# One graph-transformer kernel: joining, first norm and expert gate as one pipeline over groups of 500 nodes

## The chip, the cores and the metric

The kernel runs on one core of a Trainium2 chip. Time is the device time of one execution in microseconds, the median of several runs. The core's engines run side by side, each through its own list of instructions in order, and meet through semaphores: PE (TensorE, matrix products), DVE (VectorE), ACT (ScalarE), POOL (GpSimd; here it issues indirect DMAs) and SP (SyncE; it issues the plain DMAs).

## What is computed

3125 nodes of 256 features, 50,000 edges, two layers. Each layer adds a graph part, a mixer and a feed-forward part:

```python
xn = _layernorm(x)
x = x + _L0_gnn_ref(xn, src, dst, ...) + _L0_mix_ref(xn[None], ...)[0]   # segment_max over edges; attention and MLP
x = x + _L0_ffn_ref(_layernorm(x)[None], Wr, br, W1, ..., bo)[0]         # 8 experts, softmax gate
xn = _layernorm(x)
x = x + _L1_gnn_ref(xn, edge_index, ...) + _L1_mix_ref(xn[None], ...)[0] # 3 SAGE layers; linear attention
x = x + _L1_ffn_ref(_layernorm(x)[None], ...)[0]
```

The expert part is `w = softmax(feat @ Wr + br)`, three matrices W1, W2, Wo for each expert with relu between, and a sum over the experts weighted by w. The change lies between the end of the edge maxima and the experts.

## The kernel before

It is written in stages. Each stage is a `Scope` with a `Block`, in which every engine has its list; at its end all engines meet (L82 clears semaphores and is a barrier). Activations lie transposed, features on partitions: `c.xT`, `c.yn`, `c.a` are 128 x 2 x 3136 floats. `c.a` holds a term of the graph part and is free after the join; its two halves are then used as `c.yh` and `c.yl`, the high and low float16 part of the normalised rows in `c.yn`. A product in three float16 passes (`product3`, L814) reads these halves; `product` (L854) is a plain float32 product.

`join_max` (L713) gathers, for 25 blocks of 125 nodes, the running maxima at each node's last edge from DRAM: 25 indirect DMAs of POOL into 25 slots of `m` (L747). PE spreads carried maxima by a one-hot matrix (L795, two PSUM banks in turn), DVE takes the maximum (L773), PE transposes (L810), DVE adds `c.a`, clips and adds into `c.xT` (L785, L787), in groups of 4 blocks (500 nodes, the seventh has one block). The one-hot is made by DVE (L757) from the carry rows (L732, first in SP's queue). SP then loads the gate's and experts' small tensors and W1, W2 as floats (L734, 16 loads of 256 KB). ACT scales W1 to its high half in four pieces (L829), DVE makes the low half (L837).

`norm` (L861), called for n = 1, normalises all of `c.xT` into `c.yn`, with a software pipeline over the seven groups: mean by PE, centring (L937), square (L917), variance by PE, root (L923), reciprocal (L944), spreading by PE (L907), scaling (L949), high half (L926), low half (L954). It loads Wo. `gate` (L957) computes the logits with Wr as the stationary side, adds `br` (L994), turns them to nodes on partitions (L979), takes the softmax, turns back (L985), stores `dram.gate` (L1021) and splits W2 and Wo.

`experts` (L1025) runs 7 tiles of 448 nodes times 8 experts. `norm` 2, `split2`, `mix1` and three `sage` follow.

Beside all of it POOL writes the adjacency matrix of the later SAGE layers: 400 indirect DMAs, one for a column of cells (`place_cells`, L697, instruction L706). The calls hand fixed ranges to the stages: 0 to 8 in the join, 8 to 40 in norm 1, 40 to 64 in the gate, 64 to 330 in the experts, 330 to 350 in norm 2, 350 to 400 in mix1. A stage ends when its range is issued; the first `sage` needs all 400. DVE counts equal cells for this (L681), in the edge stage and in the experts.

## Time and profile before

| | |
|---|---|
| median of 3 runs | 2274.82 us (2274.58 to 2283.3) |
| profiled execution | 2287.81 us, span 2286.0 us |
| mean granted TensorE clock in it | 0.849 |
| busy share of the span: PE, DVE, ACT, POOL | 76%, 57%, 26%, 51% |
| DMA, mean rate over the span | 100 GB/s |

The profile is one execution recorded by the hardware. Times in it count from the span's start. A row of the order of time gives an instruction's start, its duration, the engine, the line, output and inputs, and in brackets how long the engine had stood and what released it. Edges and first mixer take the first 706 us, the part between them and the experts about 160, the experts about 450, norm 2 to mix1 about 145, the SAGE layers and the last feed-forward part the rest.

### The profile page before, as it was taken

What the parts mean: (1) busy time and instruction counts of PE and PEld (TensorE: products, weight loads), DVE (VectorE), ACT (ScalarE), POOL (GpSimd) and SP (SyncE); (2) the same over time, 40 slices, a digit from 0 to 9 for tenths busy, and PEclk for the clock granted to TensorE, in tenths of its full rate; (3) what the DMA queues carried; (4) which work ended last, traced back from release to release, by engine and by line L of the source; (5) the groups of instructions that cost most, each with busy time, mean ns of one, the idle gap of its engine ahead of it and who ended that gap; (6) DMA issues with size and microseconds to landing.
All of it is one profiled execution on the core that took longest, in us unless ns stands there. A gap on an engine that the chain in (4) does not pass through costs nothing. (4 is left out here: it accounts for less than half of the span.)

```text
span 2286.0 us, 25612 instructions
## 1 busy us (share of the span) xinstructions
PE 1742.0 (76%) x8399; PEld 1010.7 (44%) x8399; DVE 1300.6 (57%) x2567; ACT 594.1 (26%) x937; POOL 1173.6 (51%) x888
## 2 busy tenths in 40 slices
PE   7985454635552746999999259699989999997996
PEld 6862122212221513555555138655565556544543
DVE  6878666766775644777777244545541221115995
ACT  4001001100111124666666131321120010003453
POOL 0888888878886777888888857300000000000343
PEclk9557777777785868999999667899999999997998
DMA  6257688887868202111110020154424443531002
GB/s 171 62 141 196 184 222 216 216 228 211 227 191 206 60 2 51 36 34 33 33 33 13 1 66 2 19 124 108 108 50 119 126 96 92 127 79 38 1 7 78
DMA packets 193170, 229.06 MB, mean 100 GB/s; under 512 B 66574, under 2 KB 174178, under 8 KB 187697
## 3 DMA queue, kind: packets, MB, share of 16 engines
q1 hardware_dynamic: 125887, 172.58, 28.2%
q0 software_dynamic: 67200, 55.46, 11.0%
q8 instruction: 42, 0.69, 0.1%
q14 instruction: 41, 0.34, 0.0%
HBM read 148.81 MB, written 78.24 MB: 99 GB/s over the span
## 5 line engine op out<-in xcount | busy, mean ns | idle before, releaser
L706 POOL DMA_INDIRECT adjacency<-all_cell_val,all_cell_idx x400 | 546.3, 1366 | 151.2 <-issue 120.4
L273 POOL DMA_INDIRECT edge_ring<-b_rows,all_src_idx x400 | 523.9, 1310 | 174.3 <-issue 172.5
L1659 POOL TENSOR_TENSOR ffn_hl<-ffn_hid,ffn_hh 128x448 f16<-128x448 f32 x56 | 70.0, 1252 | 737.9 <-ACT ffn_hid L1676 737.9
L1472 PE MATMUL bank<-sage_adj,sage_zh 125*128 125x448 f16 x1050 | 370.1, 352 | 3.4 <-DVE sage_zl L1526 3.4
L1472 PE MATMUL bank<-sage_adj,sage_zl 125*128 125x448 f16 x1050 | 370.0, 352 | 0.0
L526 DVE SCALAR_TENSOR_TENSOR edge_ring<-edge_ring,w_keep 125x256 f32<-125x256 f32 x399 | 192.9, 484 | 142.6 <-DMA edge_ring<-b_rows,all_src_idx 122.3
L1549 DVE TENSOR_TENSOR sage_u<-bank,w_rd 128x448 f32<-128x448 f32 x42 | 26.2, 624 | 236.2 <-PE bank L1477 233.4
L1472 PEld LDWEIGHTS bank<-sage_adj,sage_zh 125*128 125x128 f16 x1050 | 102.6, 98 | 101.8 <-issue 8.0
L1472 PEld LDWEIGHTS bank<-sage_adj,sage_zl 125*128 125x128 f16 x1050 | 102.7, 98 | 99.6 <-issue 5.8
L681 DVE SCALAR_TENSOR_TENSOR edge_junk<-bank,all_key_c,all_later 125x400 f16<-125x400 f32 x232 | 145.6, 627 | 0.0
L820 PE MATMUL bank<-all_a,w_W1h 128*128 (+1 forms) x448 | 122.5, 355 | 25.0 <-ACTq L1115 25.0
L857 PE MATMUL bank<-mix_hn,w_fc 128*128 128x448 f32 x168 | 82.4, 658 | 59.4 <-DVE mix_hn L642 59.4
L857 PE MATMUL bank<-all_yn,w_qkv 128*128 128x448 f32 x56 | 39.1, 872 | 115.2 <-DVE all_xT L648 89.6
L1179 DVE TENSOR_TENSOR experts_h<-experts_h,experts_gb 128x896 f32<-128x896 f32 x56 | 61.2, 1093 | 67.7 <-ACT experts_h L1119 49.0
L917 ACT ACTIVATE norm_sq<-all_yn 128x1000 f32<-128x1000 f32 (+1 forms) x21 | 19.9, 948 | 304.1 <-DVE all_yn L937 298.5
L681 DVE SCALAR_TENSOR_TENSOR experts_junk<-all_key_c,all_later 125x400 f16<-125x400 f32 x168 | 97.5, 630 | 0.0
L1165 DVE TENSOR_TENSOR experts_h1l<-experts_hf,experts_h1h 128x896 f16<-128x896 f32 x56 | 61.2, 1092 | 63.9 <-ACT experts_hf L1119 60.4
L1119 ACT ACTIVATE experts_h1h<-bank,w_shift,w_scale 128x448 f16<-128x448 f32 x112 | 75.0, 720 | 84.9 <-PE bank L820 84.9
L1119 ACT ACTIVATE experts_h<-bank,w_shift,w_scale 128x448 f32<-128x448 f32 x112 | 75.0, 720 | 75.9 <-PE bank L820 64.1
L857 PE MATMUL bank<-all_xT,all_mean_w 128*128 128x500 f32 (+1 forms) x84 | 42.6, 644 | 62.4 <-PEq L82 62.4
L857 PEld LDWEIGHTS bank<-mix_hn,w_fc 128*128 128x128 f32 x168 | 38.7, 235 | 107.0 <-DVE mix_hn L642 68.2
L820 PE MATMUL bank<-experts_hwh,w_Woh 128*128 128x448 f16 x224 | 79.7, 356 | 2.8 <-DVE experts_hwl L1169 2.8
(423 smaller groups left out, 3598.8 us busy)
## 6 DMA issues: line engine op xcount, KB each, us to landing
sage_adj<-adjacency SPq DMA_DIRECT2D x105, 490.0 KB
run_max<-edge_ring SPq DMA_DIRECT2D x40, 1120.0 KB
adjacency<-edge_zero SPq DMA_DIRECT2D x25, 714.0 KB
experts_gb<-gate_rows SPq DMA_DIRECT2D x56, 224.0 KB
edge_ring<-b_rows,all_src_idx POOLq DMA_INDIRECT x400
adjacency<-all_cell_val,all_cell_idx POOLq DMA_INDIRECT x400
sage_adj<-adjacency SPq DMA_DIRECT2D x105, 56.9 KB
run_max<-edge_ring SPq DMA_DIRECT2D x40, 130.0 KB
```

The lines of the kernel that those rows point to most:

```text
L273: nc.gpsimd.indirect_dma_start(ring[:, k % RING, :], None, dram.rows[:, :], bass.IndirectOffsetOnAxis(ap=c.src_idx[:, k:k + 1], axis=0)).t ...
L526: v.scalar_tensor_tensor(ring[:, k % RING, :], last, w.keep[:, k:k + 1], ring[:, k % RING, :], ALU.min, ALU.max).then_inc(scanned, 1)
L681: v.scalar_tensor_tensor(junk, keys, c.key_c[:, at], c.later[:, bass.ds(L - 1 - k, L)], ALU.is_equal, ALU.mult, accum_out=c.cnt[:, at]).th ...
L706: nc.gpsimd.indirect_dma_start(dram.adj_flat, bass.IndirectOffsetOnAxis(ap=c.cell_idx[:, k:k + 1], axis=0), c.cell_val[:, k:k + 1], None). ...
L820: ins = nc.tensor.matmul(out, a, b, start=(start and i == 0), stop=(stop and i == n - 1))
L857: ins = nc.tensor.matmul(out, a, b, start=(k == 0), stop=(k == len(lhs) - 1))
L1119: return a(out, ps[bank][:, 0:T], ACT.Relu, bias=w.shift[:, i, h, e:e + 1], scale=w.scale[:, i, h, e:e + 1])
L1165: v.tensor_tensor(h1l[:, e % 2], hf[:], h1h[:, e % 2], ALU.subtract).then_inc(low1, 1)
L1179: v.tensor_tensor(h2[:, f % 2], h2[:, f % 2], gb[f][:].unsqueeze(1).to_broadcast([P, KH, T]), ALU.mult).then_inc(dm, 1)
L1472: ins = mm(ps[4 * b + h][:, 0:T], z[:, g * JG + j, half(h)], adj[g][:, j, :], start=(g == 0 and j == 0 and z is zh), stop=False)
L1549: step(v.tensor_tensor(u[:, h, :], ps[4 * b + h][:, 0:T], w.rd[:, at], ALU.mult))
L1659: nc.gpsimd.tensor_tensor(hl[:, m, :], hid[:, m, :], hh[:, m, :], ALU.subtract).then_inc(low, 1)
```

## The change

`join_max`, `norm` 1 and `gate` become one stage `join_norm_gate`. It works in turns over the same seven groups of 500 nodes: in turn t, DVE and PE join group t - 1, centre group t - 2 and scale group t - 3. The gathers go into 8 slots, and from gather 8 on POOL waits until the slot's group is turned; two columns of `place_cells` follow each such gather. The normalised rows are kept as halves only, `c.eh` and `c.el`, which lie in `c.yn`'s space; a float32 copy `y` exists for two groups. The logits are computed block by block with the rows as the stationary side, straight onto node partitions, and `br` is added there from a broadcast row. All of W1, W2 and Wo are split in this stage. The ranges of `place_cells` become 0 to 46 (`JOINED`) in this stage, 46 to 290 in the experts, 290 to 320 in norm 2, 320 to 400 in mix1. `norm` also clears the tail of its output.

The new function (semaphores, some tiles and the batch-norm and softmax arithmetic, which are as before, are cut), then the calls:

```diff
+def join_norm_gate(nc, c, dram, w, loads, plan):
+    w.total = 16 * sum(sem is w.loaded for _, _, sem in plan)
+    G4 = -(-NB // 4)
+    size = lambda g: min(4, NB - 4 * g)
+    at = lambda g: slice(4 * B * g, 4 * B * g + size(g) * B)
+    wide = lambda g: size(g) * B
+    MR = 8
+    mats, first, second = loads
+    with Scope(nc, "join") as s:
+        m = s.sb("m", [B, MR, D])
+        hot = s.sb("hot", [NONE + 1, NP])
+        t1 = s.sb("t1", [P, 4 * B])
+        y = s.sb("y", [P, 2, KH, 4 * B])
...
+        parts = first + second
...
+            def _(sp):
...
+                    sp.dma_start(hot[:, 0:N], dram.carry.partition_broadcast(NONE + 1)).then_inc(rows_in, 16)
+                    for to, from_, sem in plan:
+                        sp.dma_start(to, from_).then_inc(sem, 16)
+                    sp.dma_start(br[:], w.br_row.partition_broadcast(B)).then_inc(rows_in, 16)
+                    for n, (to, from_, sem) in enumerate(mats):
+                        if n % 2 == 0:
+                            sp.wait_ge(split_low, n // 2 + 1)
+                        sp.dma_start(to, from_).then_inc(sem, 16)
+                for k in range(2):
+                    sp.wait_ge(w_copied[k], (G4 + 1 - k) // 2)
...
+            def _(pool):
                 for j in range(NB):
+                    if j >= MR:
+                        pool.wait_ge(turned, 2 * ((j - MR) // 4) + 2)
+                    nc.gpsimd.indirect_dma_start(m[:, j % MR, :], None, dram.runs[:, :],
+                                                 bass.IndirectOffsetOnAxis(ap=c.last_idx[:, j:j + 1], axis=0)).then_inc(got[j % MR], 16)
+                    if j >= MR:
+                        place_cells(nc, c, dram, pool, 2 * (j - MR), 2 * (j - MR) + 2)
+                place_cells(nc, c, dram, pool, 2 * (NB - MR), JOINED)
...
+            def _(act):
+                act.wait_ge(w.loaded, w.total)
+                act.wait_ge(eps_ready, 1)
+                for i in range(2):
+                    nc.scalar.activation(w.bn[:, i, 4], w.bn[:, i, 4], ACT.Sqrt, bias=c.eps3[:, 0:1]).then_inc(bn_sd, 1)
+                def highs(n):
+                    src, hi, _, loaded, total = parts[n]
+                    act.wait_ge(loaded, total)
+                    nc.scalar.activation(hi, src, ACT.Copy, scale=WS).then_inc(split_high, 1)
+                for t in range(2, G4 + 3):
+                    g = t - 3
+                    if g >= 0:
+                        act.wait_ge(var_done, g + 1)
+                        if g >= 2:
+                            act.wait_ge(rs_ready, g - 1)
+                        nc.scalar.activation(sd[:, g % 2, 0:size(g)], ps[3][0:B, 0:size(g)], ACT.Sqrt, bias=c.eps5[0:B, 0:1]).then_inc(sd_ready, 1)
+                    highs(t - 2)
+                    if g >= 0:
+                        act.wait_ge(scaled, g + 1)
+                        nc.scalar.copy(c.eh[:, :, at(g)], y[:, g % 2, :, 0:wide(g)]).then_inc(high, 1)
+                    g = t - 2
+                    if g < G4:
+                        act.wait_ge(centred, g + 1)
+                        if g >= 1:
+                            act.wait_ge(var_done, g)
+                        nc.scalar.activation(sq[:, :, 0:wide(g)], y[:, g % 2, :, 0:wide(g)], ACT.Square).then_inc(sq_ready, 1)
+                for n in range(G4 + 1, len(parts)):
+                    highs(n)
+                act.wait_ge(ready, 1)
+                nc.scalar.activation(lg[:], lg[:], ACT.Exp).then_inc(ex, 1)
+                for g in range(1, G4, 2):
+                    act.wait_ge(w_turned, g + 1)
+                    nc.scalar.copy(hot[0:NEXP, at(g)], ps[g][0:NEXP, 0:wide(g)]).then_inc(w_copied[1], 1)
...
             def _(dve):
...
+                v.memset(c.eps3[:], 1e-3).then_inc(eps_ready, 1)
+                v.memset(c.eh[:, :, N:NP], 0.0)
+                v.memset(c.el[:, :, N:NP], 0.0)
+                dve.wait_ge(rows_in, 32)
+                v.memset(hot[:, N:NP], 0.0)
+                v.tensor_scalar(hot[:, 0:N], hot[:, 0:N], c.col[0:NONE + 1, 0:1], None, ALU.is_equal).then_inc(hot_ready, 1)
+                def fold_bn():
+                    dve.wait_ge(bn_sd, 2)
+                    for i in range(2):
...
+                    v.tensor_scalar(w.bo[:], w.bo[:], WS, None, ALU.mult)
+                def lows(n):
+                    src, hi, lo, _, _ = parts[n]
+                    dve.wait_ge(split_high, n + 1)
+                    v.scalar_tensor_tensor(lo, src, WS, hi, ALU.mult, ALU.subtract).then_inc(split_low, 1)
+                for t in range(G4 + 3):
+                    if t < G4:
+                        for j in range(4 * t, 4 * t + size(t)):
+                            dve.wait_ge(got[j % MR], 16 * (j // MR + 1))
+                            dve.wait_ge(spread, j + 1)
+                            v.tensor_tensor(m[:, j % MR, :], m[:, j % MR, :], ps[6 + j % 2][0:B, 0:D], ALU.max).then_inc(masked, 1)
+                    if t >= 3:
+                        g = t - 3
+                        dve.wait_ge(sd_ready, g + 1)
+                        if g >= 2:
+                            dve.wait_ge(rs_spread, g - 1)
+                        v.reciprocal(rs[:, g % 2, 0:size(g)], sd[:, g % 2, 0:size(g)]).then_inc(rs_ready, 1)
+                    if 1 <= t <= G4:
+                        g = t - 1
+                        for h in range(KH):
+                            dve.wait_ge(turned, 2 * g + h + 1)
+                            step(v.tensor_tensor(t1[:, 0:wide(g)], ps[h][:, 0:wide(g)], c.a[:, h, at(g)], ALU.add))
+                            ins = v.scalar_tensor_tensor(c.xT[:, h, at(g)], t1[:, 0:wide(g)], 0.0, c.xT[:, h, at(g)], ALU.max, ALU.add)
+                            if h == 0:
+                                step(ins)
+                        ins.then_inc(joined, 1)
+                    if t == 1:
+                        fold_bn()
+                    if t >= 3:
+                        g = t - 3
+                        dve.wait_ge(rs_spread, g + 1)
+                        for h in range(KH):
+                            ins = v.tensor_tensor(y[:, g % 2, h, 0:wide(g)], y[:, g % 2, h, 0:wide(g)], ps[4][:, 0:wide(g)], ALU.mult)
+                        ins.then_inc(scaled, 1)
+                    if 2 <= t <= G4 + 1:
+                        g = t - 2
+                        dve.wait_ge(mean_done, g + 1)
+                        if g >= 2:
+                            dve.wait_ge(logits, g - 1)
+                            dve.wait_ge(lowed, g - 1)
+                        for h in range(KH):
+                            ins = v.tensor_tensor(y[:, g % 2, h, 0:wide(g)], c.xT[:, h, at(g)], ps[2][:, 0:wide(g)], ALU.subtract)
+                        ins.then_inc(centred, 1)
+                    if t >= 3:
+                        g = t - 3
+                        dve.wait_ge(high, g + 1)
+                        dve.wait_ge(scaled, g + 1)
+                        v.tensor_tensor(c.el[:, :, at(g)], y[:, g % 2, :, 0:wide(g)], c.eh[:, :, at(g)], ALU.subtract).then_inc(lowed, 1)
+                    if t >= 3:
+                        lows(t - 3)
+                    if t >= 8:
+                        lows(t - 1)
+                dve.wait_ge(logits, G4)
+                step(v.tensor_tensor(lg[:], ps[5][0:B, 0:NB * NEXP].rearrange("p (j e) -> p j e", e=NEXP),
+                                     br[:].unsqueeze(1).to_broadcast([B, NB, NEXP]), ALU.add))
...
+                v.tensor_tensor(lg[:], lg[:], wide_mx, ALU.subtract).then_inc(ready, 1)
+                for n in range(G4 + 2, len(parts)):
+                    lows(n)
                 dve.wait_ge(ex, 1)
...
+                v.tensor_tensor(lg[:], lg[:], wide_mx, ALU.mult).then_inc(ready, 1)
+                for g in range(0, G4, 2):
+                    dve.wait_ge(w_turned, g + 1)
+                    v.tensor_copy(hot[0:NEXP, at(g)], ps[g][0:NEXP, 0:wide(g)]).then_inc(w_copied[0], 1)
...
+            def _(pe):
+                def spread_carry(j):
+                    if j >= 2:
+                        pe.wait_ge(masked, j - 1)
+                    nc.tensor.matmul(ps[6 + j % 2][0:B, 0:D], hot[:, B * j:B * (j + 1)], c.carry[:], start=True, stop=True).then_inc(spread, 1)
+                pe.wait_ge(hot_ready, 1)
+                for j in range(4):
+                    spread_carry(j)
+                for t in range(G4 + 3):
+                    if t + 1 < G4:
+                        for j in range(4 * t + 4, 4 * t + 4 + min(2, size(t + 1))):
+                            spread_carry(j)
+                    if t >= 3:
+                        g = t - 3
+                        pe.wait_ge(rs_ready, g + 1)
+                        if g >= 1:
+                            pe.wait_ge(scaled, g)
+                        for j in range(size(g)):
+                            ins = nc.tensor.transpose(ps[4][:, B * j:B * (j + 1)], rs[:, g % 2, j:j + 1].to_broadcast([B, P]), c.ident[0:B, 0:B])
+                        ins.then_inc(rs_spread, 1)
+                    if t < G4:
+                        pe.wait_ge(masked, 4 * t + size(t))
+                        if t >= 1:
+                            pe.wait_ge(joined, t)
+                        for h in range(KH):
+                            for i in range(size(t)):
+                                ins = nc.tensor.transpose(ps[h][:, B * i:B * (i + 1)], m[:, (4 * t + i) % MR, half(h)], c.ident[0:B, 0:B])
+                            ins.then_inc(turned, 1)
+                    if t >= 3:
+                        g = t - 3
+                        pe.wait_ge(scaled, g + 1)
+                        for i in range(size(g)):
+                            j = 4 * g + i
+                            ins = product(nc, ps[5][0:B, NEXP * j:NEXP * (j + 1)], [y[:, g % 2, k, B * i:B * (i + 1)] for k in range(KH)],
+                                          [w.Wr[:, k, :] for k in range(KH)])
+                        ins.then_inc(logits, 1)
+                    if 1 <= t <= G4:
+                        g = t - 1
+                        pe.wait_ge(joined, g + 1)
+                        if g >= 1:
+                            pe.wait_ge(centred, g)
+                        product(nc, ps[2][:, 0:wide(g)], [c.mean_w[:]] * KH, [c.xT[:, k, at(g)] for k in range(KH)]).then_inc(mean_done, 1)
+                    if 2 <= t <= G4 + 1:
+                        g = t - 2
+                        pe.wait_ge(sq_ready, g + 1)
+                        if g >= 1:
+                            pe.wait_ge(sd_ready, g)
+                        for j in range(size(g)):
+                            ins = product(nc, ps[3][0:B, j:j + 1], [sq[:, k, B * j:B * (j + 1)] for k in range(KH)], [c.mean_w[:, 0:1]] * KH)
+                        ins.then_inc(var_done, 1)
+                    if t + 1 < G4:
+                        for j in range(4 * t + 6, 4 * t + 4 + size(t + 1)):
+                            spread_carry(j)
+                pe.wait_ge(ready, 2)
                 for g in range(G4):
+                    for i in range(size(g)):
+                        ins = nc.tensor.transpose(ps[g][0:NEXP, B * i:B * (i + 1)], lg[:, 4 * g + i, :], c.ident[0:B, 0:B])
+                    ins.then_inc(w_turned, 1)...
@@ experts
-                                       [(c.yh[:, k, cols(t)], c.yl[:, k, cols(t)]) for k in range(KH)])
+                                       [(c.eh[:, k, cols(t)], c.el[:, k, cols(t)]) for k in range(KH)])
@@ build
-                join_max(nc, c, dram, w, plan, pieces(f[0], w.W1, mats[0]))
-                norm(nc, c, 1, lambda pool: place_cells(nc, c, dram, pool, 8, 40), [(f[0][:, e], blocks(i.Wo)[:, e], mats[2]) for e in each])
-                gate(nc, c, w, dram, pieces(f[1], w.W2, mats[1]) + pieces(f[0], w.Wo, mats[2]), lambda pool: place_cells(nc, c, dram, pool, 40, 64))
+                join_norm_gate(nc, c, dram, w, ([(f[0][:, e], blocks(i.Wo)[:, e], mats[2]) for e in each],
+                                                pieces(f[0], w.W1, mats[0]) + pieces(f[1], w.W2, mats[1]),
+                                                pieces(f[0], w.Wo, mats[2])), plan)
-            experts(nc, c, w, dram, made, lambda pool: place_cells(nc, c, dram, pool, 64, 330, made))
+            experts(nc, c, w, dram, made, lambda pool: place_cells(nc, c, dram, pool, JOINED, 290, made))
-                norm(nc, c, 2, lambda pool: place_cells(nc, c, dram, pool, 330, 350), [
+                norm(nc, c, 2, lambda pool: place_cells(nc, c, dram, pool, 290, 320), [
-            mix1(nc, c, w, qT, ctx, lambda pool: place_cells(nc, c, dram, pool, 350, L))
+            mix1(nc, c, w, qT, ctx, lambda pool: place_cells(nc, c, dram, pool, 320, L))
```

## Rows read from the trace of the kernel before

**Rows 1.** Busy us by engine (instructions), clock, DMA share, GB/s, one stretch

```profile
1280.00:1328.00 48.00, 0.42 (x1) 0.45 (x2) 0.11 (x2) 0.00 (x0) 34.96 (x30) 0.50 0.07 1
```

**Rows 2.** In order of time: the ends and beginnings of stages

```profile
873.31 0.93 PE L820 MATMUL bank<-all_a,w_W1h 128*128 128x448 f16 x2 [24.95 <-ACTq L1115]
...
1322.61 1.19 POOL L706 DMA_INDIRECT adjacency<-all_cell_val,all_cell_idx  x1 [0.30 <-issue]
...
1327.62 0.08 DVE L931 MEMSET all_a<- 128x22 f16 x1 [51.15 <-PEq L82]
...
1358.01 1.19 POOL L706 DMA_INDIRECT adjacency<-all_cell_val,all_cell_idx  x1 [0.30 <-issue]
...
1365.85 1.48 ACT L829 ACTIVATE w_glh<-staged_gl 128x1536 f16<-128x1536 f32 x1 [1.75 <-PEq L82]
...
1445.38 4.35 POOL L706 DMA_INDIRECT adjacency<-all_cell_val,all_cell_idx  x1 [0.31 <-issue]
...
1473.34 0.29 PE L820 MATMUL bank<-w_glh,all_a 128*125 128x256 f16 x1 [2.27 <-PEq L82]
```

**Rows 3.** The join's start in order of time, then its first stretch by engine

```profile
711.66 0.33 SPq L732 DMA_DIRECT2D all_yn<-carry_of  x1
...
713.70 19.36 SPq L734 DMA_DIRECT2D staged_float<-in_W  x16
...
719.99 1.85 DVE L757 TENSOR_SCALAR all_yn<-all_yn,all_col 126x3125 f32<-126x3125 f32 x1 [8.19 <-DMA all_yn<-carry_of]
...
722.98 0.51 ACT L741 ACTIVATE w_bn<-w_bn,all_eps 128x16 f32<-128x16 f32 x2 [9.82 <-DMA w_bn<-in_bn]
...
711.00:740.00 29.00, 12.55 (x44) 8.11 (x44) 13.20 (x33) 5.69 (x7) 22.37 (x18) 0.62 1.01 247
```

**Rows 4.** In order of time: first maximum and first group's transposes

```profile
726.95 0.73 DVE L773 TENSOR_TENSOR join_max_m<-join_max_m,bank 125x256 f32<-125x256 f32 x2
...
732.87 1.04 PE L810 MATMUL bank<-all_ident,join_max_m 125*128 125x125 f32 x8
```

**Rows 5.** POOL: gathers, their landing, columns by stretch, one column in the gate

```profile
L747 POOL DMA_INDIRECT join_max_m<-run_max,all_last_idx x25: 1207/1211/2220, 712.4 to 750.9; - x25
...
DMA to landing us min/median/max: 4.0/4.3/9.1
...
1276.40:1323.80 47.40, 37.95 (x32) 0.53 0.07 1
...
874.00:1276.40 402.40, 331.06 (x235) 0.99 0.16 33
...
828.86 9.61 POOL L706 DMA_INDIRECT adjacency<-all_cell_val,all_cell_idx  x1 [0.30 <-issue]
```

**Rows 6.** DVE by line, join then norm 1: count, busy us, mean ns, idle

```profile
L773 DVE TENSOR_TENSOR join_max_m<-join_max_m,bank 125x256 f32<-125x256 f32 x25 | 10.1, 418 | 9.2 <-PE bank L795 6.5 <-DMA join_max_m<-run_max,all_last_idx 2.5
L787 DVE SCALAR_TENSOR_TENSOR all_xT<-join_max_t,all_xT 128x500 f32<-128x500 f32 (+1 forms) x14 | 8.7, 624 | 0.5
...
L837 DVE SCALAR_TENSOR_TENSOR w_W1l<-staged_float,w_W1h 128x1024 f16<-128x1024 f32 x4 | 4.9, 1218 | 0.0
...
L937 DVE TENSOR_TENSOR all_yn<-all_xT,bank 128x500 f32<-128x500 f32 (+1 forms) x14 | 8.0, 615 | 5.6 <-PE bank L857 5.6
...
L954 DVE TENSOR_TENSOR all_a<-all_yn,all_a 128x1000 f16<-128x1000 f32 (+1 forms) x7 | 7.5, 1082 | 0.0
```

**Rows 7.** PE in norm 1, in order of time: variance, means, variance again

```profile
779.25 1.80 PE L857 MATMUL bank<-all_mean_w,norm_sq 128*125 128x1 f32 x16
...
781.37 1.84 PE L857 MATMUL bank<-all_xT,all_mean_w 128*128 128x500 f32 x4
...
795.36 3.52 PE L857 MATMUL bank<-all_mean_w,norm_sq 128*125 128x1 f32 x16 [1.97 <-ACT norm_sq L917]
```

**Rows 8.** The gate's end: PE's transposes, and SP's wait for the store

```profile
842.99 5.37 PE L985 MATMUL bank<-all_ident,gate_lg 125*8 125x125 f32 x25 [3.93 <-DVE gate_lg L1006]
...
SPq L969 <- DMA gate_rows<-gate_wT: 2.9, 1, 2.9
```

More of the change, by code:

```diff
@@ new lines, in _ @@
+            @block.sync
+            def _(sp):
+                with nc.allow_non_contiguous_dma(reason="weights in blocks of 128 rows"):
+                    sp.dma_start(hot[:, 0:N], dram.carry.partition_broadcast(NONE + 1)).then_inc(rows_in, 16)
[8 more added lines that the diff above has]
+                    sp.wait_ge(w_copied[k], (G4 + 1 - k) // 2)
+                sp.dma_start(dram.gate[:, :], hot[0:NEXP, :]).then_inc(gate_stored, 16)
+                sp.wait_ge(gate_stored, 16)
```

171 lines of the change are left out of this document (32 added, 139 removed).

## The prediction, made before the change was run

> **What bounds the kernel now.** I read the page's time slices first, then the busy time by stretch, then the order of time around each stage's end. The reader should look for the engine that works last in each stage, because every stage ends in a barrier that all engines must reach. From the first join to the first SAGE layer that engine is mostly POOL, which writes the 400 adjacency columns by `place_cells`. After the experts' compute comes a stretch of 48 us in which PE is busy 0.42 us, DVE 0.11 and POOL 34.96 [rows 1]; POOL's last issue there is at 1322.61, and norm 2's first DVE work at 1327.62 [rows 2]. Norm 1 and the gate end on POOL in the same way. From POOL's last end (1322.61 + 1.19) to the next stage's work I count 3.6 us, rounded down from 3.8 for the stages whose engines start sooner. Norm 2 and mix1 end on compute: POOL is through at 1359.2 and 1449.7, the next stages start at 1365.85 and 1473.34 [rows 2]. So POOL has 400 columns to write between 711.7 and 1473.3, and a compute gain in this part counts only where it isn't behind POOL.
>
> The stretches that the change touches, by their starts: join, norm 1 and gate 711.7 to 873.3, 161.6 us; experts 873.3 to 1327.6, 454.3; norm 2 to 1365.9, 38.3; split2 and mix1 to 1473.3, 107.5.
>
> **Columns moved after the experts.** Columns by stage before and after: join to gate 64 and 46, experts 266 and 244, norm 2 20 and 30, mix1 50 and 80. One column costs 1.49 us where nothing disturbs it (47.4 us for 32) and 1.71 us beside the experts (402.4 us for 235) [rows 5].
>
> Experts: 244 columns. 234 of them fit beside the compute as now, 10 follow: the 22 that go were all in the 47.4 us tail, so 22 x 1.49 = 32.8 us less. Ten columns (14.9 us) still stand behind the compute, so the cut is taken in full. Reading `eh`, `el` out of another buffer costs the experts' matmuls nothing: same shapes, same order.
>
> Norm 2: ten more columns put POOL's end at 1359.2 + 14.9 + 0.5 for DVE's interference = 1374.6 on the old time line, the next stage 3.6 later at 1378.2 instead of 1365.9: +12.3. A 22-column memset is nothing.
>
> Mix1: thirty more put POOL's end at 1449.7 + 44.7 = 1494.4. POOL's column at 1445.38 took 4.35 us, 3.2 over its 1.19, beside a whole-tile DVE subtraction (L1299) [rows 2]; the product of the same shape at L1304 now also meets columns. Between 0 and 3.2 more, I take 2.6, as about 80% of starts would be caught: 1497.0, plus 3.6 = 1500.6 against 1473.3: +27.3.
>
> Together -32.8 + 12.3 + 27.3 = **+6.8**, between +3 and +10. It is a transfer from a stage with 47 us of bare POOL into two that had 6 and 24 us of room.
>
> **The merged stage.** It has no barrier inside (the two releases at norm and gate go), a shorter logits path, and its own order. I follow the last chain.
>
> Start: DVE's one-hot waits for `rows_in` 32, which counts the carry rows and `br`. `br` is now issued behind the 16 loads of W1 and W2. Those issues ran from 713.70 for 19.36 us, against a full queue [rows 3]. Ahead of `br` lie 1.58 MB of carry rows, 4.19 MB of weights and, now, only 8 gathers (1.02 MB) and 0.1 MB of small loads: 6.9 MB. The first 29 us moved 247 GB/s, 7.2 MB [rows 3], so 6.9 MB are through at about 739. The carry rows alone were in at 719.99, when the one-hot began. That small loads wait behind large ones is seen in `w_bn`: issued at about 713.3, it let ACT go at 722.98 [rows 3]. The Trainium skill (DMA: Bandwidth & Descriptors, Queues, rings and completion order) says that each engine takes descriptors in ring order, while completion is not in order per issuing engine; by the first half `br` lands at 739, and `w_bn` agrees; by the second it might come a little before the last weights.
>
> One-hot 1.85 us, to 741. Then four spreads and maxima, two spreads and eight transposes. Before, the same work with two more spreads took from 726.95 (first maximum, which had waited for the batch-norm fold) to 733.9 [rows 4]; with the first spread and less two, about 6 us: group 0 is turned at 747. POOL has issued gathers 0 to 7 by 725 and stands still for 22 us, as gather 8 waits for `turned` 2.
>
> POOL's pace: from gather 8 two columns follow each gather, so gather 23 is issued 15 gathers (1.51 us: 1.21 and 0.30) and 30 columns (1.49) later: 67.4 us. DVE's split and low passes hold POOL up: one column took 9.61 us in the gate [rows 5]. Four L837 in the join cost POOL some 0.8 each. Zero to 8 us; I take 3, three turns with such passes. With 4.3 us to land [rows 5], group 5 is whole at 747 + 67.4 + 3 + 4.3 = 821.7. The pace is 12 instructions, some 18.5 us, a group, while DVE has about 11 us of work in a turn and PE 9 at full clock, 17 at half: both are hidden before this point.
>
> After it DVE still has, from [rows 6]: 2 maxima 0.8; the join of groups 4 and 5 (four operations of 0.7 each with their steps, 2.8) and of the short group 6 (1.4), 7.0; scaling, priced like centring, 4 x 1.25 + 0.5 = 5.5; centring 3 x 1.25 + 0.5 = 4.3; `el` 4 x 1.2 + 0.4 = 5.2; seven weight pieces of 1.2, 8.4; five small reciprocals some 0.8: 32 us. Then three weight pieces 3.6 and six short operations of the softmax some 2.3, 5.9; transposes and copies 6.1 (5.37 on PE alone), store and landing 3.2 (2.9 of waiting) [rows 8], block end some 1.1: 16.3 us. If DVE never waited the experts would begin at 870.0. It does wait: `spread_carry` 4t+6 stands behind logits, mean and variance on PE, and the next reciprocal needs the variance through ACT. From the join's end PE has transposes 1.0, logits 1.8 (same form as the 16 variance passes), mean 1.8, variance 1.8 [rows 7]: 6.5 us against DVE's 5.0 at the upper clock (2.4 GHz), 12 to 13 at the lower (1.2). That is 5 us over turns 5 to 8 at the one and about 20 at the other. The 16 variance passes took 1.80 us in a dense stretch and 3.52 right after PE had stood 1.97 us [rows 7]. Turns 2 to 5 each begin with PE waiting for a gather; later turns are dense. I take 10.
>
> The experts begin at 821.7 + 32 + 10 + 16.3 = 880.0, and some 0.5 us of hand-overs, 880.5 against 873.3: **+7**. POOL itself is through at 747 + 63 x 1.5 + 6 = 847.5 and no longer holds this stage. So the barriers, two norm-to-gate releases and 12.7 us of POOL's lag at the norm are saved, and given back as 19 us of later start, POOL's pace for gathers, and a serial tail.
>
> The Trainium skill (TensorE: Matmul & The Clock Gate, What's actually happening) says that the throttled state is the default and that activity releases it. By it a pipeline paced by gathers would run its PE part at the lower level, which is the rival "lower clock" below.
>
> **Sum.** +7.2 + 6.8 = +14. All of it is made against the profiled execution, 2287.81 us with a span of 2286.0, which is 0.57% above the median of the runs, 2274.82; taken as a difference on the median it gives **2289**.
>
> **Rivals.** (1) *Lower clock*: PE stays at 1.2 GHz through the tail. The second variance row of [rows 7] is such a spell, and the new stage makes PE wait for gathers in four turns. The tail costs 20 in place of 10, and the starved POOL may add: 2298. (2) *DVE hides PE*: upper clock and ready data from turn 5; the stage ends at 870 to 873, -3 to 0, with +6.8 for the columns: about 2280, not slower by over 0.5%. It decides if PE's granted clock is above 0.9 from the last full gather on. (3) *`br` is not held*: the other side. If with fewer gathers in the way SP issues the weight loads without a full queue, and `br` lands beside the carry rows at 722, everything up to the tail moves by 17, and with the tail of (2) the experts begin at 853: -20 + 7 = -13, 2262. It decides from a landing before 730. Against it: 4.19 MB must be issued first, and the queue filled in the trace. (4) That the merge doesn't do what it says: POOL's columns would bind the stage as before. With 63 instructions from 747 they end at 848, 32 us ahead, so this holds only if POOL is starved by over 30 us: 2290 and up, no separate case.
>
> **Chances.** Forecast (2282 to 2296) 0.45, lower clock 0.22, DVE hides PE 0.2, `br` early 0.1, rest 0.03. A measurement tells 0.5% (11.4 us) from no change. The forecast case lies across that bound (2286.2), two thirds above it: slower 0.45 x 0.65 + 0.22 + 0.02 = 0.53; faster, most of the `br` case, 0.09; same 0.38. The range leaves out the lower part of `br` early and the top of the lower clock: 2266 to 2306.
>
> **What would show it.** In the changed kernel: the one-hot starts at 737 to 742 (27 us after the carry load's issue); POOL stands 20 us before its ninth gather; full groups land every 18 us or so; the stage from its first issue to the first expert matmul takes 169 us; the experts stage takes 421 to 422, norm 2 about 50, split2 and mix1 135. Wrong would be: a start before 730, PE done early in every turn of the tail, columns at other than 1.49 us, or mix1 ending on compute in spite of 80 columns.

## Result and profile after

| | before | after |
|---|---|---|
| runs beside each other | 2275.46 us median of 4 (2274.58 to 2283.3) | 2309.7 us median of 4 (2308.84 to 2310.49) |
| ratio | | 1.0143, 95% interval 1.0124 to 1.0163 |
| profiled execution | 2287.81 us, span 2286.0 | 2310.27 us, span 2308.5 |

The changed kernel is slower by 1.4%, 34 us. The forecast was 2289 with a range of 2266 to 2306: the direction is right, the size is not, and the time lies above the range. The kernel before varies more than four runs show: in the later comparisons, one beside each group of experiments, its median was 2282.45, 2280.09, 2278.31 and 2275.67 us, and over all its 42 executions 2279.2. Against that the changed kernel is 30 us slower. Differences below between medians of different comparisons carry some us of this.

The stages of the changed kernel in order of time. These rows answer to [rows 2, 3]: the carry load's issue, `br`'s, the one-hot, gather 8, POOL's last column of the stage, the store of the gates, the experts' first load, POOL's last columns before norm 2, norm 2, split2, mix1's first work, DVE's last work in it, its last column, DVE's first work in SAGE, and SAGE's first cast.

```profile
709.66 0.33 SPq L899 DMA_DIRECT2D join_hot<-carry_of  x1
...
730.64 0.70 SPq L902 DMA_DIRECT2D join_br<-in_br  x1
...
737.01 1.83 DVE L970 TENSOR_SCALAR join_hot<-join_hot,all_col 126x3125 f32<-126x3125 f32 x1 [27.12 <-issue]
...
744.96 1.21 POOL L917 DMA_INDIRECT join_m<-run_max,all_last_idx  x1 [22.69 <-PE bank L1083]
...
838.67 1.40 POOL L707 DMA_INDIRECT adjacency<-all_cell_val,all_cell_idx  x1 [0.30 <-issue]
...
882.06 0.32 SPq L909 DMA_DIRECT2D gate_rows<-join_hot  x1
886.21 0.30 SPq L1143 DMA_DIRECT2D experts_gT<-gate_rows  x1
...
1306.56 1.18 POOL L707 DMA_INDIRECT adjacency<-all_cell_val,all_cell_idx  x1 [0.30 <-issue]
...
1311.88 0.08 DVE L831 MEMSET all_a<- 128x22 f16 x1 [22.38 <-PEq L83]
...
1361.69 1.48 ACT L729 ACTIVATE w_glh<-staged_gl 128x1536 f16<-128x1536 f32 x1 [14.08 <-PEq L83]
...
1367.31 1.96 ACT L1328 ACTIVATE mix_xr<-all_yn 128x1000 f32<-128x1000 f32 x2 [2.76 <-PEq L83]
...
1459.49 1.03 DVE L1412 TENSOR_SCALAR w_ctx<-bank,mix_sums 32x32 f32<-32x32 f32 x4 [5.46 <-PE bank L1474]
...
1490.55 1.18 POOL L707 DMA_INDIRECT adjacency<-all_cell_val,all_cell_idx  x1 [0.30 <-issue]
...
1496.92 0.17 DVE L1605 TENSOR_SCALAR sage_b<-w_gbias 128x2 f32<-128x2 f32 x1 [36.40 <-PEq L83]
...
1498.47 0.37 ACT L1588 CAST sage_zh<-bank 125x256 f16<-125x256 f32 x1 [53.87 <-PE bank L720]
```

DVE had waited 22.4 us for norm 2's first work and 36.4 us, from mix1's last at 1460.5, for SAGE's: both stages before them end on POOL. The merged stage does not: POOL is through at 840 and the stage goes on for 46 us.

Three traces of the kernel before were taken in all, and they differ. Stages from row to row as above (SAGE from its first cast), in us:

| kernel | join to gate | experts | norm 2 | split2, mix1 | from SAGE on | span |
|---|---|---|---|---|---|---|
| before, first trace | 161.6 | 454.4 | 38.2 | 108.8 | 811.4 | 2286.0 |
| before, second trace | 162.0 | 454.3 | 38.2 | 103.1 | 810.7 | 2280.2 |
| before, third trace | 161.9 | 452.7 | 37.5 | 100.3 | 807.8 | 2272.5 |
| after | 176.6 | 425.7 | 49.8 | 136.8 | 810.0 | 2308.5 |

Against the third trace, whose time (2274.27) is that of before's median, the change costs 14.7 us in the merged stage, gains 27.0 in the experts, costs 12.3 in norm 2 and 36.5 in split2 and mix1, and 2.2 behind; the join begins 2.6 us sooner. Sum 36.1, of 36.0 measured between the spans. The last two are no effect of the change: over all traces of all versions the join begins at 708.4 to 712.3 us, and the part from SAGE on takes 807.5 to 812.3.

How the merged stage's tail goes, from the last big group on: DVE's reciprocals, one for each group, PE's variance passes of the first turn, and its passes of the second.

```profile
817.55 0.17 DVE L1002 RECIPROCAL join_rs<-join_sd 125x4 f32<-125x4 f32 x1
...
828.96 3.36 PE L757 MATMUL bank<-all_mean_w,join_sq 128*125 128x1 f32 x16
...
832.66 0.18 DVE L1002 RECIPROCAL join_rs<-join_sd 125x4 f32<-125x4 f32 x1 [7.31 <-ACT join_sd L942]
...
836.77 3.52 PE L757 MATMUL bank<-w_Wr,join_y 128*125 128x8 f32 x16 [0.43 <-DVE join_y L1018]
...
840.15 3.68 PE L757 MATMUL bank<-all_xT,all_mean_w 128*128 128x500 f32 x4
...
843.62 2.25 PE L757 MATMUL bank<-all_mean_w,join_sq 128*125 128x1 f32 x16
...
846.21 0.18 DVE L1002 RECIPROCAL join_rs<-join_sd 125x4 f32<-125x4 f32 x1 [6.07 <-ACT join_sd L942]
...
856.83 0.18 DVE L1002 RECIPROCAL join_rs<-join_sd 125x4 f32<-125x4 f32 x1 [4.70 <-ACT join_sd L942]
...
866.28 0.16 DVE L1002 RECIPROCAL join_rs<-join_sd 125x1 f32<-125x1 f32 x1
```

The busy time by stretch. Columns: stretch and length, busy us (instructions) of PE, PEld, DVE, ACT, POOL, then the granted clock, DMA share and GB/s. The first row is a turn paced by gathers, the other four are the turns of the tail.

```profile
782.00:800.00 18.00, 14.01 (x57) 10.60 (x56) 8.63 (x15) 3.27 (x4) 14.35 (x13) 0.59 0.27 59
...
817.50:832.70 15.20, 12.85 (x48) 10.42 (x48) 7.79 (x14) 2.40 (x4) 11.96 (x10) 0.50 0.21 45
832.70:846.20 13.50, 10.85 (x42) 8.03 (x42) 7.34 (x11) 3.22 (x5) 6.14 (x5) 0.56 0.17 40
846.20:856.80 10.60, 8.38 (x40) 8.06 (x40) 5.82 (x11) 3.25 (x5) 0.00 (x0) 0.58 0.00 0
856.80:866.30 9.50, 5.46 (x24) 4.98 (x24) 5.32 (x9) 3.49 (x5) 0.00 (x0) 0.50 0.01 2
```

DVE is busy for 26.3 us of these 48.8, PE for 37.5. The clock is at its lower level, 0.50, in the first and last of these turns, and its mean is 0.56 and 0.58 in the other two, so that it is at the upper level for a small part of them, although PE works for 85% of the first turn. The 16 variance passes that took 1.80 us at the upper level [rows 7] take 3.36 in the first turn and 2.25 in the second, where the clock rises during them. The waits of DVE in this stretch, in us in total, times, longest:

```profile
DVE join_rs L1002 <- ACT join_sd L942: 18.1, 3, 7.3
DVE join_m L996 <- DMA join_m<-run_max,all_last_idx: 3.7, 1, 3.7
DVE w_W2l L989 <- ACT w_W2h L934: 2.3, 1, 2.3
```

The 3.7 us ended at 817.21, with the landing that made the last big group whole, and lie ahead of the tail. ACT's square root waits in its turn for the variance passes, so the 18.1 us are PE's.

### The profile page after: what moved, and what is told of

Same layout as the page of the kernel before. It is cut to its first block and busy times, and to the rows that moved or that the text cites. A ratio compares the mean times of both kernels' runs of the same rounds, so it can differ in the third digit from the quotient of the medians.

```text
span 2308.5 us, 25665 instructions
## 1 busy us (share of the span) xinstructions
PE 1757.6 (76%) x8446; PEld 1031.0 (45%) x8446; DVE 1294.3 (56%) x2559; ACT 596.4 (26%) x940; POOL 1162.0 (50%) x888
## 5 line engine op out<-in xcount | busy, mean ns | idle before, releaser
L707 POOL DMA_INDIRECT adjacency<-all_cell_val,all_cell_idx x400 | 538.5, 1346 | 182.6 <-issue 121.0
L720 PE MATMUL bank<-all_yn,w_W1h 128*128 (+1 forms) x448 | 123.6, 358 | 4.7 <-ACTq L1207 4.7
L1271 DVE TENSOR_TENSOR experts_h<-experts_h,experts_gb 128x896 f32<-128x896 f32 x56 | 61.2, 1093 | 67.5 <-ACT experts_h L1211 67.4
L720 PE MATMUL bank<-w_glh,all_a 128*125 128x256 f16 x300 | 55.3, 291 | 50.8 <-PEq L83 50.8
L720 PE MATMUL bank<-all_yn,w_W1l 128*128 (+1 forms) x224 | 80.1, 358 | 0.0
```

Source lines behind the costliest of these rows:

```text
L707: nc.gpsimd.indirect_dma_start(dram.adj_flat, bass.IndirectOffsetOnAxis(ap=c.cell_idx[:, k:k + 1], axis=0), c.cell_val[:, k:k + 1], None). ...
L720: ins = nc.tensor.matmul(out, a, b, start=(start and i == 0), stop=(stop and i == n - 1))
L1271: v.tensor_tensor(h2[:, f % 2], h2[:, f % 2], gb[f][:].unsqueeze(1).to_broadcast([P, KH, T]), ALU.mult).then_inc(dm, 1)
```

## The experiments

My theory behind the result: the merged stage's tail is bound by PE at the lower clock; the late `br` shifts the whole stage; the columns moved behind the experts cost what POOL needs for them; and the forecast's base, one trace of before, was too high in mix1.

**1. The kernel before again, twice.** No edit.

> The kernel before, unchanged, for a second trace. Its first trace took 2287.81 us, 12 us over the median of its runs. Theory A (stall of POOL): that trace has a column of the gate that took 9.61 us beside DVE's weight pieces, which other executions lack; a trace of an execution near 2275 us then shows no column over 3 us in the gate, and the experts begin 9 to 12 us earlier than 873.3. Theory B (clock): the 12 us are spread over the SAGE layers or the last feed-forward part, at a lower granted clock; the gate is then the same within 2 us.

Measured: 2281.98 us. Its gate has the long column too (9.49 us), so that stall is no peculiarity of one execution, and theory A fell. Theory B did too: from SAGE on the two traces differ by 0.7 us. Only mix1 differs, by 5.7 us.

> The kernel before, unchanged, for a third trace of it: its first profiled execution took 2287.8 us where the median of the runs beside the changed kernel was 2275.5, and the second 2282.0. Theory: an execution of it that lies lower is shorter in mix 1, whose products run at a higher granted clock there (103 us from the first of mix 1 to the first cast of SAGE in the first trace, 97.5 in the second), and begins the join up to 3 us earlier; the merged stages' neighbours (gate 162, experts 454, norm 2 38) stand within 1 us. Rival: the gate or the experts vary, by GpSimd's long column (9.6, 9.5 and 8.4 us so far).

Measured: 2274.27 us. Split2 and mix1 take 100.3 us, the long column is there again:

```profile
830.10 9.31 POOL L706 DMA_INDIRECT adjacency<-all_cell_val,all_cell_idx  x1 [0.30 <-issue]
```

The place of the theory is right, mix1 (8.5 of the 13.5 us), and its cause is wrong. 8.0 of the 8.5 us lie in one stretch, from ACT's first copy at L1246 to DVE's reduction at L1290: 25 products of eight passes each go into two banks in turn, which DVE and ACT copy out. It takes 29.2 us in the first trace, 23.1 in the second and 21.2 in the third, at a granted clock of 1.00 in all three. What differs is PE: it is busy 23.9 of 29.5 us, 22.1 of 23.2 and 20.8 of 21.2, so it stands still for 5.6, 1.1 and 0.4 us, in part until DVE has copied a bank out, and its passes take 3 us longer in the first than in the third. Why one execution has this rhythm and another not stays open. The join began at 712.27, later and not earlier; 3.6 us are behind SAGE's first cast, and 1.6 and 0.8 in the experts and norm 2. Six traces with 80 columns in mix1 (after and experiments 2, 3, 6, 7 and 8) put it at 136.4 to 137.3 us. Before's mix1 ends on compute and varies by 8 us; the changed one ends on POOL and doesn't.

**2. `br` ahead of the weight loads.**

```
-                    sp.dma_start(br[:], ...)    # behind the 16 weight loads
+                    sp.dma_start(br[:], ...)    # behind the carry rows
```

> The changed kernel with the load of br issued right behind the carry rows, ahead of the weights. Theory A (late start): DVE's one-hot starts near 718 to 720 instead of 737, and the whole chain (first group turned, POOL's gathers, tail) moves with it: the experts begin 16 to 18 us earlier, the kernel takes 2309.7 - 17 = 2293 us. Theory B (POOL or the weight loads bound the stage): the gathers from 730 on meet the weight loads and land in 9 us instead of 4, or the weight pieces are late; less than 8 us are won.

Measured: 2294.34 us (2292.88 to 2296.28), ratio 1.0051 (1.0035 to 1.0068): 15.4 us less than the changed kernel. The one-hot's row, 10.6 us behind the carry load's issue in place of 27.4:

```profile
722.14 2.06 DVE L970 TENSOR_SCALAR join_hot<-join_hot,all_col 126x3125 f32<-126x3125 f32 x1 [10.41 <-issue]
```

The stage takes 161.9 us, what the three stages took before, so without the late bias the merge costs nothing and gains nothing. Up to the first reciprocal 16.0 us are won (55.4 us from the carry load's issue in place of 71.5); the second turn of the tail gives 1.1 back, since it ran at 0.50 in place of 0.56.

**3. The new column ranges without the merge.** The kernel before, with 290 and 320 as the ends of the experts' and norm 2's columns.

> The kernel before with only the column ranges after the gate changed: 64 to 290 in the experts, 290 to 320 in norm 2, 320 to 400 in mix1. Theory A (account of columns): the experts end on compute at once, 454.3 - 50 = 404; norm 2 is longer by 12, mix1 by 27.7: -10 us together, 2265 us. Theory B (the later ranges cost nothing by themselves, since columns are hidden behind mix1): -50 us, 2225 us. Theory C (they only cost): +39 us.

Measured: 2278.11 us (2275.75 to 2280.39), ratio 0.998 (0.997 to 0.9989), 4.5 us less. Stages 160.5, 405.5, 50.6, 136.6: the experts gain 49 us since 40 columns leave them (POOL is through with the 226 at 1261.9, and the compute goes on to 1276.7), and norm 2 loses 12 and mix1 28 to 36, by the trace of before that it is set against.

**4. The merge with the old ranges** (64, 330, 350).

> The changed kernel with the column ranges of the kernel before (64 columns in the gate stage, up to 330 beside the experts, up to 350 beside norm 2, the last 50 beside mix 1), so that it differs from the kernel before by the merged stage alone. Theory (the merged stage costs what its two traces say, and the new ranges cost the rest because 244 columns are left to the experts, more than fit beside their products): the merged stage again 176.6 us (the 18 more columns, 1.7 us each, end near 869, before the gates are stored), experts 454, norm 2 38, split and mix 1 107, so 10.7 us less than the changed kernel by these stages: 2299 us, ratio near 1.010; up to 5 less if mix 1, no longer bound by GpSimd, runs faster than in the first trace of before. Rival (GpSimd binds the merged stage as soon as it has more columns, as it did with 76): the stage grows to 190 us or more and the time is at least 2310.

Measured: 2297.55 us (2296.31 to 2298.79), ratio 1.0075 (1.0058 to 1.0092). Stages 176.7, 458.3, 37.8, 103.6. POOL's 64 columns end at 871, ahead of the gates' store at 884.4, so they were free in the merged stage. The changed kernel lies 12.2 us above this one: it takes 18 columns out of the merged stage, where they cost nothing, and 22 out of the experts (-32.6 us), and puts the 40 into norm 2 (+12.0) and mix1 (+33.2). The experts take 4 to 6 us more here than before with the same 266 columns: beside a compute of 403 us POOL issues 232 or 233 in the traces of the merged kernels that have so many to issue, and 235 or 236 before. What holds it up by those three I can't say.

**5. 76 columns in the merged stage** (then 306, 328).

> The changed kernel with columns 0 to 76 in the merged stage, 76 to 306 in the experts, 306 to 328 in norm 2, 328 to 400 in mix1. POOL stood 47 us at the end of the merged stage. Theory A (that idle is free): the merged stage stays at 177 us, the experts end on compute (403 to 406, -20 to -22), norm 2 is 11 us shorter, mix1 12 to 16: 2309.7 - 46 = 2264 us. Theory B (columns beside the tail hold DVE or PE up): the merged stage grows by 5 us or more and the sum is over 2270 us.

Measured: 2273.26 us (2271.14 to 2275.08), ratio 0.9958 (0.9942 to 0.9975), 9 us more than I expected, and 36.4 less than the changed kernel: by the traces 19.7 less in the experts, 11.4 in norm 2 and 12.0 in mix1, and 5.3 more in the merged stage. The gates are stored at 884.12, but POOL's last column holds the stage, and the next one begins after it:

```profile
889.01 1.19 POOL L707 DMA_INDIRECT adjacency<-all_cell_val,all_cell_idx  x1 [0.30 <-issue]
894.41 1.19 POOL L707 DMA_INDIRECT adjacency<-all_cell_val,all_cell_idx  x1 [4.21 <-POOLq L83]
```

The stage takes 181.9 us, the experts 406.0, which is compute: 230 columns are through beside it. With the 232 counted above that is what fits beside the experts. For the merged stage I estimate 72, from 5.3 us at 1.49 a column.

**6. Half of PE's logits and variance passes.** The second half of the features is left out of both products, so logits and variances are not the reference's.

```
-  product(nc, ps[3][0:B, j:j + 1], [sq[:, k, ...] for k in range(KH)], ...)
+  product(nc, ps[3][0:B, j:j + 1], [sq[:, 0, ...]], ...)    # logits alike
```

> The changed kernel in which the logits' and the variances' products take the first of the two halves of 128 features only (the second is left out, so half of these passes of TensorE). VectorE, ScalarE and GpSimd do all that they did. Theory (behind the last big group TensorE at the lower clock binds: 12.3 us busy of a 14 us turn): each full turn loses 3.4 us, the five logits and three variances behind 817 lose about 1.7 us each, so the tail of 68.6 us becomes 55 and the kernel some 13 us faster, 2297 us. Rival (the chain of handovers between ScalarE and VectorE binds, TensorE fills its gaps): under 4 us less, 2306 or more. The halved products may also lower the granted clock further where it is between the levels; it cannot in the tail, which is at the lower level already.

Measured: 2299.54 us (2298.25 to 2302.81), ratio 1.0089 (1.0072 to 1.0106), 10.2 us less; the stage takes 164.6 us, 12.0 less. The paced turns keep their 18.1 to 18.3 us. The turns of the tail shrink from 15.1, 13.5, 10.6 and 9.5 to 11.4, 10.7, 7.3 and 7.4:

```profile
830.96 0.18 DVE L1002 RECIPROCAL join_rs<-join_sd 125x4 f32<-125x4 f32 x1 [3.58 <-ACT join_sd L942]
...
841.62 0.18 DVE L1002 RECIPROCAL join_rs<-join_sd 125x4 f32<-125x4 f32 x1 [3.03 <-ACT join_sd L942]
```

From the last big group on PE is busy 12.7 us less, partly because the clock is a little higher (0.54, 0.68, 0.65, 0.50), and the four turns take 12.0 us less. So PE's passes set the length of the tail. That its clock does too stands in the kept traces: the same second turn, with the same passes, took 14.67, 14.65 and 14.66 us at 0.50 (experiment 2 and the last two versions of 9), 13.5 at 0.56 (after) and 13.1 at 0.58 (experiment 8). No trace has a tail at the upper level throughout.

**7. Filler passes to raise the clock.**

```
+  pe.wait_ge(high, 1)      # behind the wait for the last scaling, from the fifth turn on
+  for i in range(5):
+      nc.tensor.matmul(ps[4][:, 0:400], c.eh[:, 0, 0:P], c.eh[:, 0, 0:400], start=True, stop=True)
   pe.wait_ge(rs_ready, g + 1)
```

> The changed kernel with five further products of 128 x 400 halves on TensorE in each turn from the fifth on, written to the bank of the spread 1/sd between its last reader and its next transpositions, that is in the time in which the engine would wait for the reciprocal: 2000 columns a turn, 0.83 us at 2.4 GHz, 1.7 us at 1.2 GHz. Theory (the tail is long because the clock stays at its lower level under passes of few columns): the granted clock behind 817 rises above 0.6, the turns shorten, the time falls by 5 to 20 us. Rival (the granted clock doesn't answer to this filler): clock 0.50 there as before, the fillers displace 0 to 1.7 us in each of four or five turns, the time 2309 to 2317.

Measured: 2316.16 us (2313.72 to 2334.18), ratio 1.0191 (1.0146 to 1.0236). The clock of the tail did not answer: 0.50, 0.56, 0.58 and 0.50 in its four turns, as without the fillers, with PE busy 13.18 of 15.10, 12.24 of 13.50, 9.03 of 10.62 and 8.23 of 10.32 us. In the paced turn ahead, the first with fillers, the clock was 0.68, where the changed kernel has 0.59, but in the paced turn before that one, without fillers, it was 0.50 against 0.59. The first row is the filler between the first and the second of these turns, the second the busy time of the first.

```profile
836.03 1.83 PE L1075 MATMUL bank<-all_yn 128*128 128x400 f16 x5
...
821.40:836.50 15.10, 13.18 (x50) 10.62 (x51) 7.69 (x13) 2.35 (x4) 12.10 (x10) 0.50 0.22 46
```

The first two tail turns stayed at 15.1 and 13.5 us. The filler ahead of the first ran at 817.89, while PE stood waiting for DVE and DVE for a gather. The one ahead of the second, 1.83 us, fitted into PE's waits there: in the trace of after 0.57 us for the reciprocal and 1.70 for DVE's four joining passes, which lie ahead of the scaling. So the turn is a loop (reciprocal, transposes, scaling, logits, means, variances, square root) in which PE at the lower clock is busy for all but 2 to 3 us (12.85 of 15.20, 10.85 of 13.50), and not a queue of PE work without a gap. Neither of my two expectations said that. The stage took 178.9 us, 2.3 more: 1.0 in the last paced turn, 0.9 in the last turn of the tail, 0.6 at the start. The rest of the 6.5 us between the medians I can't place; two of the four executions took 2313.7, one 2318.57, and one 2334.18 at a mean clock of 0.805 where the others have 0.834 to 0.838. What raises the clock in such a stretch stays open. The Trainium skill (TensorE: Matmul & The Clock Gate, What's actually happening) says that activity releases the throttle; what the profile counts as 12.24 us of 13.50 busy didn't keep it released here. An earlier form of the filler, eight passes of 256 columns a turn into the carry products' banks, gave no time: nothing orders those passes against DVE's reads of the same banks.

**8. One column behind each gather in place of two.**

```
-  place_cells(nc, c, dram, pool, 2 * (j - MR), 2 * (j - MR) + 2)
+  place_cells(nc, c, dram, pool, j - MR, j - MR + 1)
```

> The changed kernel with one column issued behind each gather in place of two (17 in place of 34), the other 17 behind the last gather; 46 columns in the stage as before. The last gather is then issued 25.5 us sooner. Theory (the middle turns are paced by GpSimd at 18.1 us for four gathers and eight columns, while TensorE needs 14 us of them at the lower clock): the turns from the second to the fifth shorten to 14 to 16 us, the stage by 7 to 18 us, the time 2298 us (2291 to 2303). Rival (TensorE and VectorE need the 18 us anyway, as in the tail): less than 4 us off, over 2305.

Measured: 2298.28 us median of 5 (2287.17 to 2307.09), ratio 1.0088 (1.0061 to 1.0116). 11.4 us less, as expected, but with a spread of 20 us, which otherwise only experiment 7 had, by one execution. In the profiled execution (2287.17, the fastest) the stage takes 155.4 us, 21.2 less where I expected 7 to 18, since two of its turns ran at a higher clock than the theory had. The clock shows a way to such a spread. The same turn (56 to 58 passes), first in this kernel, then in two turns of the kernel of experiment 9 with this pace:

```profile
784.30:795.60 11.30, 10.55 (x58) 7.80 (x57) 8.81 (x17) 3.27 (x4) 9.17 (x8) 0.85 0.34 81
```

```profile
756.00:773.20 17.20, 16.20 (x56) 12.66 (x56) 8.86 (x17) 3.27 (x4) 13.72 (x12) 0.50 0.31 76
773.20:785.70 12.50, 11.49 (x57) 8.05 (x56) 8.75 (x16) 3.27 (x4) 10.06 (x9) 0.77 0.32 74
```

A full turn takes 17.1 us at 0.50 and 11.3 to 12.5 at 0.77 to 0.85. With the old pace of 18.1 us POOL hid this (in experiment 2 a full turn took 18.2 us at 0.50 and 18.4 at 0.59); at the new one PE decides, and with it the clock. The five executions' mean clocks fit: 0.843 and 0.844 at 2287.17 and 2290.28 us, 0.838 and 0.836 at 2298.28 and 2299.24, 0.833 at 2307.09. That the whole spread comes from these turns is argued, not shown: only one execution of this kernel has a trace.

**9. Versions built on this.** `br` first and the columns divided 66, 298, 333:

> The changed kernel with the DMA of the router's bias issued ahead of the 16 weight loads, and the columns divided as 66 in the merged stage, up to 298 beside the experts (232, what fits beside their products), up to 333 beside norm 2 (35, at about 1.43 us a column beyond 22), and the last 67 beside mix 1 (at 80 it was bound by GpSimd; the slope from 80 to 72 columns, 2.2 us a column, meets the compute at about 67). From the traces: merged stage 162, experts 406, norm 2 57, split and mix 1 107.5, together 732.5 against 749.6 with 76 columns in the merged stage and the bias late (2273.3 us): 2256 us, ratio 0.989. If the 66 columns hold the end of the merged stage as the 76 did, 2260 to 2270.

Measured: 2264.25 us (2263.34 to 2266.03), ratio 0.9931 (0.9914 to 0.9948). Merged stage 160.4, experts 407.8, norm 2 58.4, split2 and mix1 117.0: 9.5 us over in mix1, which is still bound by POOL's 67 columns. Then one column behind each gather as well:

> The kernel with the bias issued first and the columns divided 66/298/333 (2264.3 us), with one column behind each gather in place of two. If pace binds the middle turns as a_pace1 supposes: the stage 150 us in place of 160.5, GpSimd's last column still near 856, the time 2254 us (2248 to 2258). If TensorE binds them: 2261 to 2265.

Measured: 2256.16 us (2255.24 to 2258.38), ratio 0.99 (0.9883 to 0.9916). The gates are stored 16 us sooner than in the version above (851.44 against 867.66), and the stage ends 9 us sooner (862.72), now on POOL's last column at 857.82. At last three columns in POOL's first wait:

> The kernel with the bias first, one column behind each gather and the columns 66/298/333 (2256.2 us), with three further columns in the 4.5 us in which GpSimd waits for the first turn, ahead of gather 8, so that mix 1 keeps 64 in place of 67. Theory (GpSimd issues without a pause from the join to mix 1's last column, so each column put into one of its waits is worth 1.5 us): 4.5 us less, 2252 us. Rival (the three columns' writes and issues delay gather 8, and every group behind it): 2255 to 2258.

Measured: 2254.47 us (2251.09 to 2255.06), ratio 0.9904 (0.9887 to 0.992). In the traces mix1 is 5.2 us shorter and the merged stage 0.6 longer, as expected; against before, 21.2 us in place of 22.2, the times don't show it. What is left between the two is below what they can tell. Both beat the kernel before by 1%. From the join's second turn to the end of mix1 POOL pauses in them only where stages meet: some 4 to 5 us at two places, and 10.0 between its last column in norm 2 and its first in mix1, with `split2` in between.

## Why the prediction was wrong, point by point

- **Start.** Right. `br` was held behind the weight loads: one-hot 27.4 us after the carry load's issue (27 forecast), gather 8 at 744.96 after a wait of 22.7 (22 forecast). `br` first brings the one-hot 16.7 us nearer to the carry load (experiment 2), where 8.3 us lay between them before.
- **POOL's pace.** Right, and even without the 3 us of stall that I added: 67.4 us forecast; the last big group was whole at 817.2, 107.5 us after the stage's beginning, where 110.0 was forecast.
- **The tail.** This is the first step that failed: "I take 10" for DVE's waits for PE. From 817.5 to 866.3 DVE is busy 26.3 us, where I had 32 for it, and idle 22.5, of which 19.3 end with PE's work (18.1 through ACT's square root, 1.2 for a spread reciprocal) and 3.0 with ACT's own. The end behind it took 19.9 us, where I had 16.3 and 0.5. Waits +12.5, DVE -5.7, end +3.1, pace -2.5: +7.4, and the stage 176.6 for 169. The mechanism stood in rival (1), *lower clock*, with 20 for this term. I had read that turns from the sixth on are dense, and took dense for upper clock; the trace of after has PE at 85% and the clock at 0.50. PE's price at the lower clock was right (12 to 13 us from the join's end forecast, 12.3 measured in the first turn). The two variance rows in [rows 7] didn't say what decides between the levels, so this rival deserved more than 0.22.
- **Experts.** -28.7 in place of -32.8: 12 columns stood behind the compute, not 10 (232 beside it, not 234). The size of one column held; from 266 to 244 columns in the merged kernel (experiment 4) the experts lose 32.6 us.
- **Norm 2.** +11.6 in place of +12.3, right.
- **Mix1.** +28.0 in place of +27.3 against the first trace, and +36.5 against the third. The columns' price held. This is the second step that failed, the one sentence with which the sum passes from the profiled execution to the median: that a difference against an execution 12 us over the median can be "taken as a difference on the median". The excess lay for the most part (8.5 us) in mix1, on compute, nearly all of it in one stretch of products at a granted clock of 1.00 (experiment 1); 80 columns put POOL there, and what a quicker execution gains on compute is then lost. The difference was +22.5 between the first spans and +34 between the medians. A part of the 12 us is chance in the base itself, since 2274.82 was the median of three runs and all 42 executions have 2279.2; how large a part of the 34 that is can't be told.
- **The range.** It ended at 2306; these two terms together are about 7 and 12 us, and the forecast with both is 2308. Rival (1) alone gave 2298.
- **Rival (3)** has its condition unmet (no landing before 730) and its price confirmed: the stage of experiment 2, with `br` there at 722, is 14.7 us shorter (17 forecast), though its tail is that of rival (1). Rivals (2) and (4) didn't occur: the clock was below 0.9 and POOL was done 46 us before the stage's end.

## What to carry to other kernels

Give a stage that ends in a barrier as much background work as its critical engine hides, and no more: 64 columns were free in the merged stage, 46 left 12 us lying, and 76, with the later ranges to match, cost the stage 5 us and made the kernel 36 us faster than 46 did. A small load on which the first instruction waits belongs ahead of the large ones on its queue. Where a change turns a compute-bound stage into one bound by something else, forecast it against several executions, since what the old stage won or lost from one to the next goes with it.

## What the runs showed of the hardware

- The granted clock stayed at 0.50 through turns with PE busy 12.85 of 15.20 us, and 13.18 of 15.10 in the kernel with fillers (0.56 with 12.24 of 13.50, where a whole filler of 2000 columns lay right ahead), yet stood at 0.85 in a turn of 11.3 us with the same sort of passes.
- One column on POOL took 9.61, 9.49, 9.31 and 8.38 us in the gate of four traces with the old three stages. In the first of them DVE made six split passes and five additions of `br` meanwhile, one right behind the other. In the merged stage the split passes mostly come singly, and no column took over 1.4 us in the changed kernel or over 2.24 in any version.
- POOL needs 1.49 us for a column in all of these kernels where nothing holds it up, 1.71 to 1.74 beside the experts, and some 4 us from its last one in a stage to its first in the next (889.01 + 1.19 to 894.41).
